# A step of a static schedule moved: the last normalisation's transposes, the router product and the routing steps stand 28 to 36 ticks later

## The chip, the cores and the metric

The kernel runs on one core of one Trainium2 chip. The metric is the device time of one execution in microseconds. Five engines work side by side, each through its own list of instructions in order: TensorE (PE, with its weight loads shown as PEld), VectorE (DVE), ScalarE (ACT), GpSimd (POOL) and SyncE (SP), which here issues most DMAs. They meet only in semaphores.

## The reference

16 sequences of 128 rows and 256 columns pass through two layers, each an attention-like mixer and a feed-forward part, all with residual additions:

```python
x = x + _L0_xattn_ref(_layernorm(x), k, bias, ctx, ctx, 8)          # long convolution of ctx * v, gated
x = x + _L0_ffn_ref(_layernorm(x), W, bias, rw1, ..., A, B, gates)  # dense + top-2 of 16 low-rank experts
x = x + _L1_xattn_ref(_layernorm(x), ctx, wq, ..., wp, bp)          # 16-head attention, q and out int8-quantised
x = x + _L1_ffn_ref(_layernorm(x), router_w, expert_bias, gate_w, up_w, down_w, shared...)
```

The last part is the one that the change is about. Each of the 2048 tokens is normalised, a router product of 32 columns gives scores sqrt(softplus(logits)), the four best of 32 experts (by score plus bias) are taken, and the output is the weighted sum of their clamped SwiGLU results plus that of a shared expert:

```python
logits = flat @ router_w.T
scores = jnp.sqrt(jax.nn.softplus(logits))
_, idx = jax.lax.top_k(scores + expert_bias, K)          # K = 4, E = 32
topv = jnp.take_along_axis(scores, idx, axis=1); topv = topv / (topv.sum(-1, keepdims=True) + 1e-20)
out = sum over e of p[:, e] * ((silu(clip(flat @ wg.T)) * clip(flat @ wu.T)) @ wd.T)  + shared expert
```

## The kernel before, in words

The work is cut into 16 blocks of 128 tokens (b = 0 to 15). A block goes through everything up to the router in one long software pipeline; then all tokens are scattered to lists by expert in HBM, gathered again as 95 tiles of 128 rows of one expert each, multiplied, scattered back and summed.

The order of the pipeline is written out by hand in tables of numbers. Every engine's program runs the same loop over ticks (t = 0 to 5785), and each step stands at a first tick and repeats at a fixed distance: 128 ticks for what is done once a block, 32 for what is done four times a block, 32 also for the shared expert (SD), and at T + GOFF[g] for the five routing groups (blocks 0 to 3, 4 to 7, 8 to 11, 12 to 14, 15; GOFF is 0, 512, 1024, 1408, 1536). Ticks are no time: they only fix the order of the steps on one engine, since each step first waits for its semaphores. Two steps of one tick stand in the order of the code.

The steps that matter here, with their lines:

- xC (DVE L796, L800) adds the attention's output to x and takes the statistics stD; rsD (POOL L1239 to L1243) makes the factor; xnD (ACT L1058) normalises; xd (ACTq L1080) writes the rows four times to HBM.
- xnTD (PE L452, L453) transposes xnD, x4 (ACT L1181) copies the result out of its PSUM bank, rp (PE L459) is the router product, lg (DVE L805) copies the logits.
- routing of a group: ra (ACT L1199, L1201: Abs, Exp), rb (DVE L836), rc (ACT L1205: Ln), rd (DVE L840 to L857), re (ACT L1209: Sqrt), top (DVE L861 to L880), mb (DVE L887 to L894), rk (PE L492, L493), cum (DVE L902 to L917), which yields the index lists ixl. Exp and Tanh, Ln, and Sqrt need different tables on ACT; the switch shows as ACT_TABLE_LOAD.
- the list (POOL L1313): 64 indirect DMAs that scatter a staged block of rows to the experts' lists. SP loads the seven staging slots (L1371) and before that fills the lists with 32 writes of 2 MB (L1350); the first load waits for all of them.
- softmax of the attention: S (PE L537), mx (DVE L791), P (ACT L1164), PP (PE L523, transposes), PT (ACT L1156, the copy), pv (PE L508, which needs PT), oT (ACT L1171), oP (PE L516), oi (DVE L779 to L627, quantiser), oiP (PE L437, L438), oiT (ACT L1176), op (PE L445).
- the long convolution: kv (POOL L1299), conv (PE L557, in a single bank), z (DVE L773), uT (PE L346, L348). The low-rank experts: pa (L375), rl (L370), wx (DVE L741), wxp (PE L382), wb (PE L388, L392), xB (DVE L747).
- the shared expert, from tick 2652 on: xr (PE L466), x5 (ACT L1186), gu (PE L478), sc (DVE L810, L813), th (ACT L1191), hh (DVE L818), dn (PE L486), acc (DVE L822).

PSUM banks are handed out in PE's order from a ring of four; a PE step waits until the reader of what was in its bank four steps before is done.

Of the kernel before, what the change touches and what calls it, by code (L numbers as in the profile page):

```python
# [93 lines left out]
def build(nc, a_x, a_ctxT, a_tk, a_pack, a_qp, a_rows, a_w, a_dest, a_pad, out):  # L94
    ctx = ExitStack()
    with ctx:
        def sb(name, shape, dt=F32):
            return ctx.enter_context(nc.sbuf_tensor(name, shape, dt))
# [24 lines left out]
        def cutter(base):  # L123
# [18 lines left out]
        z = [carve([128, 2048]) for _ in range(3)]  # L142
# [12 lines left out]
        xi = [carve([128, 256]) for _ in range(2)]  # L155
# [3 lines left out]
        v = [carve([128, 16, 32]) for _ in range(3)]  # L159
# [6 lines left out]
        x4 = [carve([128, 256]) for _ in range(2)]  # L166
# [5 lines left out]
        rb = [carve([128, 4, 256]) for _ in range(4)]  # L172
# [3 lines left out]
        th = [carve([128, 2, 128]) for _ in range(3)]  # L176
        hT = [carve([128, 128]) for _ in range(2)]
        y = [carve([128, 256]) for _ in range(4)]
        xr = [tk[:, 8 + b, :] for b in range(4)]
        x5 = [tk[:, b, :] for b in range(2)]  # L180
        sc = [tk[:, 12 + b, :] for b in range(2)]
# [8 lines left out]
        lg = [sb(f"lg{i}", [128, 80]) for i in range(2)]  # L190
# [23 lines left out]
        mb = sb("mb", [128, RG * NE], BF16)  # L214
# [4 lines left out]
        cum = sb("cum", [128, NB + 1, NE])  # L219
# [68 lines left out]

        T_PE = {"wsc": 555, "xnTA": 235, "uT": 574, "xnTB": 757, "h": 780, "rl": 802, "pa": 811, "wxp": 831,
# [3 lines left out]
        T_DVE = {"swb": 533, "mvA": 66, "sk": 400, "xA": 583, "mvB": 711, "hb": 785, "e2": 806, "wx": 813,  # L293
# [3 lines left out]
        T_ACT = {"vT": 240, "xT": 760, "eh": 783, "e2": 819, "wxT": 831, "kz": 924, "xiT": 893, "qT": 992,  # L297
            "P": 1011, "oiT": 1168, "x4": 1196, "x5": 2658, "th": 2679, "ra": 1592, "rc": 1603, "re": 1668,
            "oT": 1137, "xnA": 212, "xnB": 747, "xnD": 1190, "xd": 1196, "shw": 2459, "xr": 2571,
            "xnC": 878, "q": 923, "PT": 1035}  # L300
        T_POOL = {"rsA": 131, "rsB": 699, "rsC": 827, "rsD": 1170, "vc": 315, "us": 415, "kv": 296, "xb": 818,
# [1182 lines left out]
```

How the kernel before makes its waits and increments, by code:

```python
        def tensor_program(pe):  # L309
            pe.wait_ge(d_id, 16)
            for t in range(TICKS):
                for n in at(t, T_PE["wsc"], 16, 2):
                    p, free = banks.take(("wint", n), s_wint, n + 1)
                    pb = p[:, :].bitcast(BF16)
                    pe.wait_ge(*free)
                    pe.wait_ge(s_const, 1)
                    pe.wait_ge(s_wq, n + 1)
                    for c in range(2):
                        for k in range(2):
                            o = 256 * k + 128 * c
                            i = pe.transpose(pb[:, o:o + 128], wtb[:, 256 * c + 128 * k:256 * c + 128 * k + 128], idb[:, :])
                    i.then_inc(s_wqT, 1)
                    if n == 0:
                        continue
                    p, free = banks.take(("swb", n), s_swb, 1)
                    pe.wait_ge(*free)
                    pe.wait_ge(s_pconst, 1)
                    for c in range(2):
                        i = pe.matmul(p[:, 128 * c:128 * c + 128], ones[:, :], wdg[:, c, :], start=True, stop=True)
                    i.then_inc(s_wsc, 1)
                for b in at(t, T_PE["xnTA"], 128, NB):
                    p, free = banks.take(("vT", b), s_vT, b + 1)
                    pe.wait_ge(*free)
                    pe.wait_ge(s_xn["A"], b + 1)
                    pe.transpose(p[:, 0:128], xnA[0][:, 0:128], ident)
                    pe.transpose(p[:, 128:256], xnA[0][:, 128:256], ident).then_inc(s_xnT["A"], 1)
```

## Time and profile before

| | |
|---|---|
| three runs | 724.69, 725.38, 725.76 us (median 725.38) |
| the profiled execution | 728.71 us, its span 726.9 us |
| busy in the span | PE 579.1 us (80%), DVE 482.2 (66%), ACT 379.5 (52%), POOL 373.7 (51%) |
| PE clock granted, mean | 0.922 of full |
| HBM | 53.92 MB read, 100.28 MB written |

A profile row gives a start and a duration; what stands in brackets is how long the engine had been idle before, and what released it. A busy share is a mean over stages: the pipeline of blocks lasts to about 496 us, the rest of the list to 530, the expert tiles to 685, the summing to the end. PE's recorded durations overlap, since matmuls are pipelined: the distance of two starts is what one costs.

### The profile page before, as it was taken

To read this page: it belongs to the slowest core of one execution; us is meant where nothing else is said; L and a number is where in the kernel's file an instruction comes from. 1 tells how busy PE (TensorE), PEld (TensorE's weight loads), DVE (VectorE), ACT (ScalarE), POOL (GpSimd) and SP (SyncE) were. 2 spreads that over 40 slices of the span, in tenths; PEclk is the share of its full clock that TensorE was granted. 3 is DMA by queue.
4 is the path that set the end of the run, shared out by engine and by line. 5 is a ranking of instruction groups with operands and counts; after the bars stand their busy time and mean duration, and the time that the engine had idled before them with its cause. 6 is when DMAs were issued, how large, how long until landed. Compare 5 with 4: busy or idle time off the path is not lost.

```text
span 726.9 us, 14275 instructions
## 1 busy us (share of the span) xinstructions
PE 579.1 (80%) x4045; PEld 467.2 (64%) x4045; DVE 482.2 (66%) x1462; ACT 379.5 (52%) x1107; POOL 373.7 (51%) x526
## 2 busy tenths in 40 slices
PE   1588899999969966986998779973069999999920
PEld 1487788777758855775786556652058878888810
DVE  1646657777897753789657796677437776555587
ACT  1002456666765542782757765673036666666610
POOL 6757847564472536874316521054715555555550
PEclk9999999999988986997999989996569999999975
DMA  8989999999999964321004990269535555555688
GB/s 279 218 214 334 335 334 332 334 325 317 317 317 328 307 206 139 119 67 52 30 17 145 334 330 29 74 187 343 178 110 159 162 158 157 158 161 161 208 278 277
DMA packets 135740, 155.02 MB, mean 213 GB/s; under 512 B 15248, under 2 KB 124944, under 8 KB 135408
## 3 DMA queue, kind: packets, MB, share of 16 engines
q1 hardware_dynamic: 117536, 122.50, 56.8%
q0 software_dynamic: 7632, 20.98, 8.0%
q10 hardware_dynamic: 10496, 10.62, 4.6%
q8 instruction: 36, 0.59, 0.4%
q14 instruction: 40, 0.33, 0.2%
HBM read 53.92 MB, written 100.28 MB: 212 GB/s over the span
## 4 chain that ended last, share of the span: by engine, by line
PE 39%; SPq 31%; DMA 12%; DVE 9%; issue 4%; ACT 2%; POOL 2%; ACTq 0%; DVEq 0%; POOLq 0%
SPq L1350 28%; PE ps L605 11%; PE pS L578 6%; PE pc L557 3%; DMA stage<-in_pad 3%; DMA expert_rows<-stage 3%; DMA work<-y_rows 2%; SPq L1333 2%; PE pS L537 2%; DMA expert_rows<-stage,ixl 2%; PE ps L478 2%; PE ps L348 2%; PE ps L523 1%; PE po L597 1%; DVE xs L1048 1%
## 5 line engine op out<-in xcount | busy, mean ns | idle before, releaser
L1323 POOL DMA_INDIRECT y_rows<-tk,work x95 | 94.1, 990 | 81.8 <-ACT tk L1231 74.9
L557 PE MATMUL pc<-arena,tk 128*128 128x128 f32 x768 | 109.2, 295 | 15.8 <-DVE arena L773 8.5
L557 PEld LDWEIGHTS pc<-arena,tk 128*128 128x128 f32 x768 | 97.4, 203 | 28.7 <-DVE arena L773 15.0
L1299 POOL TENSOR_TENSOR arena<-arena 128x512 f32<-128x512 f32 x64 | 90.4, 1430 | 19.8 <-ACT arena L1099 19.5
L605 PE MATMUL ps<-arena,work 128*128 x380 | 99.8, 386 | 0.3 <-ACT work L1226 0.3
L985 DVE TENSOR_SCALAR work<-ps 128x256 f32<-128x256 f32 x95 | 40.2, 423 | 67.9 <-PE ps L605 67.3
L1313 POOL DMA_INDIRECT expert_rows<-stage,ixl x64 | 63.7, 995 | 35.6 <-DMA stage<-xn_rows 17.9
L1164 ACT ACTIVATE work<-pS,work 128x128 f32<-128x128 f32 x256 | 72.5, 370 | 3.7 <-DVE work L791 3.7
L605 PEld LDWEIGHTS ps<-arena,work 128*128 128x128 f32 x380 | 66.0, 194 | 5.9 <-issue 0.7
L578 PE MATMUL pS<-arena,tk 128*128 x190 | 59.6, 395 | 2.2 <-ACT tk L1221 2.1
L791 DVE TENSOR_REDUCE work<-pS 128x4 f32<-128x512 f32 x64 | 43.8, 685 | 26.3 <-PE pS L537 26.2
L773 DVE TENSOR_TENSOR arena<-pc,arena 128x512 f32<-128x512 f32 x64 | 43.5, 680 | 24.6 <-PE pc L557 24.6
L1216 ACT ACTIVATE tk<-work 128x128 f32<-128x128 f32 x95 | 29.4, 309 | 56.6 <-DVE work L985 51.4
L1239 POOL TENSOR_TENSOR stD<-stD,epsc 128x1 f32<-128x1 f32 x16 | 3.0, 188 | 91.1 <-DVE stD L618 91.1
L523 PE MATMUL ps<-pk,work 128*128 128x128 f32 x256 | 39.5, 277 | 3.5 <-ACT work L1164 1.5
L578 PEld LDWEIGHTS pS<-arena,tk 128*128 128x128 f32 x190 | 28.3, 188 | 19.5 <-issue 10.5
L1156 ACT ACTIVATE work<-ps 128x512 f32<-128x512 f32 x64 | 37.8, 591 | 3.1 <-PE ps L523 1.6
L1231 ACT ACTIVATE tk<-pS 128x256 f32<-128x256 f32 x95 | 37.1, 390 | 3.5 <-DMA y_rows<-tk,work 3.5
L537 PE MATMUL pS<-arena,work 32*128 32x256 f32 x256 | 37.2, 408 | 0.2 <-ACT work L1149 0.2
L348 PE MATMUL ps<-pk,arena 128*128 128x128 f32 x256 | 36.8, 295 | 0.0
L523 PEld LDWEIGHTS ps<-pk,work 128*128 128x128 f32 x256 | 30.0, 142 | 7.4 <-issue 2.1
L348 PEld LDWEIGHTS ps<-pk,arena 128*128 128x128 f32 x256 | 33.5, 156 | 0.0
(271 smaller groups left out, 1369.0 us busy)
## 6 DMA issues: line engine op xcount, KB each, us to landing
expert_rows<-stage SPq DMA_DIRECT2D x32, 2080.0 KB, 21.7
work<-expert_rows SPq DMA_DIRECT2D x95, 130.0 KB, 2.2
arena<-in_w SPq DMA_DIRECT2D x8, 1536.0 KB, 14.7
stage<-xn_rows SPq DMA_DIRECT2D x64, 130.0 KB, 2.4
xn_rows<-xnD ACTq DMA_DIRECT2D x16, 512.0 KB, 7.5
work<-y_rows SPq DMA_DIRECT2D x16, 512.0 KB, 5.2
tk<-in_tk SPq DMA_DIRECT2D x1, 2048.0 KB, 9.3
out<-xs SPq DMA_DIRECT2D x16, 128.0 KB, 3.2
```

The costliest lines, as they stand in the source:

```text
L348: i = pe.matmul(pv, zv[:, k, :], ident, is_transpose=True, start=False, stop=(k == 7))
L523: i = pe.transpose(p[:, 128 * k:128 * k + 128], Pt[m % 3][:, 128 * k:128 * k + 128], ident)
L537: i = pe.matmul(p[:, 256 * c:256 * c + 256], qT[b % 3][r, 128 * c:128 * c + 128], kz[b % 3][r, c, :, :].rearrange("p a b -> p (a b)"), sta ...
L557: i = pe.matmul(pv, tk[:, h, 128 * d:128 * d + 128], kvv[:, ci, :, :].rearrange("p b (i h j) -> p (b i) h j", i=8, h=8)[:, :, hl, :], star ...
L578: i = pe.matmul(p[U * k:U * k + U, 0:256], hT[n % 2][:, U * k:U * k + U], arena[:, 512:][:, bass.ds(e, 256)], start=True, stop=True)
L605: i = pe.matmul(p[U * k:U * k + U, 0:256], xgT[n % 3][:, 128 * c + U * k:128 * c + U * k + U], arena[:, 256 * c:][:, bass.ds(e, 256)], sta ...
L791: dve.tensor_reduce(mx[:, g, :], sbanks.place["S", m][:, :].rearrange("p (k m) -> p k m", k=4), AX.X, ALU.max, negate=True).then_inc(s_mx, 1)
L1164: i = act.activation(Pt[m % 3][:, 128 * k:128 * k + 128], sbanks.place["S", m][:, 128 * k:128 * k + 128], ACT.Exp, bias=mx[:, g, k:k + 1])
L1299: pool.tensor_tensor(kv[kk % 4][:, c, half, :].rearrange("p (i h j) -> p i h j", h=8, i=8), i0, i1, ALU.mult).then_inc(s_kv, 1)
L1313: pool.indirect_dma_start(out=Xs, out_offset=bass.IndirectOffsetOnAxis(ap=ixl[:, b, k:k + 1], axis=0), in_=stage[:, j % NS, :], in_offset= ...
L1323: pool.indirect_dma_start(out=Yr, out_offset=bass.IndirectOffsetOnAxis(ap=xg[n % NX][:, 256:257].bitcast(U32), axis=0), in_=y[n % 4], in_o ...
L1350: sp.dma_start(Xs[e * NB * 128:(e + 1) * NB * 128, :].rearrange("(j p) d -> p j d", p=128), stage[:, e % 4, :].unsqueeze(1).broadcast_to(( ...
```

## The change

Only numbers in four tables are different; no instruction is added or removed. For instance on PE:

```diff
-            "xnTD": 1196, "rp": 1201, "xr": 2652, "gu": 2663, "dn": 2738, "rk": 1724, "pv": 1038, "PP": 1025,
+            "xnTD": 1228, "rp": 1236, "xr": 2652, "gu": 2679, "dn": 2754, "rk": 1752, "pv": 1038, "PP": 1025,
```

In full: PE xnTD +32, rp +35, gu and dn +16, rk +28. DVE lg +36, sc, hh and acc +16, rb and rd +32, top, mb and cum +28, ta +30. ACT x4 +33, th +16, ra +30, rc +32, re +28. POOL and SP keep their orders; so do xnD, xd and x5 on ACT and xr on PE. xnTD moves from before the third of a block's four pv steps to before the fourth, behind uT, wxp, PP and wb.

On DVE, routing group 1, where block 8's attention output is added (xC, L796). Before:

```order
L791 TENSOR_REDUCE work<-pS1 128x4
L861 RECIPROCAL rt<-rt 128x128
L863 TENSOR_TENSOR rt<-rt 128x128
L865 TENSOR_TENSOR rt<-rt 128x128
L867 TENSOR_SCALAR rt<-rt 128x128
L869 TENSOR_TENSOR rt<-rt,rows 128x128
L873 MAX m8<-rt 128x8 x4
L877 MAX_INDEX i8<-m8,rt 128x8 x4
L880 CAST f8<-i8 128x32
L690 TENSOR_REDUCE s16_0<-arena 128x32
L704 SCALAR_TENSOR_TENSOR arena<-arena 64x128
L796 SCALAR_TENSOR_TENSOR work<-ps3,work,swb 128x256
```

After:

```order
L796 SCALAR_TENSOR_TENSOR work<-ps3,work,swb 128x256
L800 TENSOR_TENSOR xs<-xs,work 128x256
L616 BN_STATS stD<-xs 128x6
L618 BN_AGGR stD<-stD 128x2
L773 TENSOR_TENSOR arena<-pc,arena 128x16x32
L791 TENSOR_REDUCE work<-pS0 128x4
L714 SCALAR_TENSOR_TENSOR lg1<-ps3,lgb 128x16
L717 MAX lg1<-lg1 128x8
L719 TENSOR_TENSOR lg1<-lg1 128x1
L720 MAX_INDEX ix1<-lg1 128x8
L722 TENSOR_TENSOR lg1<-rows,ix1 128x32
L861 RECIPROCAL rt<-rt 128x128
```

The top-4 cluster (L861 to L880) stood between mx and xC; now xC and its statistics come first, and the cluster stands behind the top-2 choice of block 11 (L714 to L722), ahead of that block's wx.

On ACT, the same group, around the Ln of rc (L1205) and the PT copies (L1156). Before:

```order
L1199 ACTIVATE rt<-lg4 128x128
L1201 ACTIVATE rt<-rt 128x128
L1121 ACTIVATE work<-ps2 128x256
L1205 ACT_TABLE_LOAD
L1205 ACTIVATE rt<-rt 128x128
L1156 ACTIVATE work<-ps3 128x512
L1164 ACT_TABLE_LOAD
L1164 ACTIVATE work<-pS1,work 128x128 x4
L1058 ACTIVATE xnA0<-xs,stA 128x256
L1149 ACTIVATE work<-ps1,bq4,wsm 128x128 x2
L1058 ACTIVATE xnB0<-xs,stB 128x256
L1156 ACTIVATE work<-ps3 128x512
```

After:

```order
L1181 ACTIVATE work<-ps3 128x256
L1164 ACTIVATE work<-pS1,work 128x128 x4
L1058 ACTIVATE xnA0<-xs,stA 128x256
L1199 ACTIVATE rt<-lg4 128x128
L1201 ACTIVATE rt<-rt 128x128
L1149 ACTIVATE work<-ps0,bq4,wsm 128x128 x2
L1205 ACT_TABLE_LOAD
L1205 ACTIVATE rt<-rt 128x128
L1058 ACTIVATE xnB0<-xs,stB 128x256
L1156 ACTIVATE work<-ps3 128x512
```

ra, rc and the Ln table load stood before the PT copy and P of the third quarter; now they stand behind that P, around qT (L1149), ahead of xnB and the PT copy of the fourth quarter. x4 (L1181) stands directly before P.

On DVE, the quantiser oi of block 13 (L779 to L627) and the shared expert's sc (L810, L813), hh (L818) and acc (L822). Before:

```order
L818 SCALAR_TENSOR_TENSOR tk<-tk 128x128
L822 SCALAR_TENSOR_TENSOR xs<-ps2,xs 128x256
L779 RECIPROCAL work<-ps3 128x16
L781 TENSOR_TENSOR work<-ps3,work 128x256
L621 TENSOR_REDUCE work<-work 128x1
L623 TENSOR_SCALAR work<-work 128x1
L625 RECIPROCAL work<-work 128x1
L627 TENSOR_SCALAR work<-work 128x256
L791 TENSOR_REDUCE work<-pS1 128x4
L810 TENSOR_SCALAR tk<-ps3 128x256
L813 TENSOR_TENSOR tk<-tk 128x128
```

After:

```order
L627 TENSOR_SCALAR work<-xnC0,work 128x256
L810 TENSOR_SCALAR tk<-ps3 128x256
L813 TENSOR_TENSOR tk<-tk 128x128
L779 RECIPROCAL work<-ps1 128x16
L781 TENSOR_TENSOR work<-ps1,work 128x256
L621 TENSOR_REDUCE work<-work 128x1
L623 TENSOR_SCALAR work<-work 128x1
L625 RECIPROCAL work<-work 128x1
L627 TENSOR_SCALAR work<-work 128x256
L791 TENSOR_REDUCE work<-pS1 128x4
L818 SCALAR_TENSOR_TENSOR tk<-tk 128x128
L822 SCALAR_TENSOR_TENSOR xs<-ps2,xs 128x256
```

hh and acc stood before oi and sc behind it; now it is the other way round.

## Rows read from the trace of the kernel before

**Rows 1.** The chain that ended last, in order of time: start us, us, what
```profile
251.98 19.70 DMA expert_rows<-stage
...
274.61 1.19 POOL expert_rows L1313
```

**Rows 2.** Stages: us, busy of each engine, PEclk, DMA share, GB/s
```profile
303.20:335.80 32.60, 26.13 (x203) 21.52 (x203) 27.62 (x74) 20.83 (x50) 25.42 (x32) 0.91 0.28 85
...
403.00:428.80 25.80, 19.15 (x149) 14.22 (x149) 21.36 (x73) 21.32 (x53) 12.36 (x20) 1.00 1.01 381
...
456.10:474.50 18.40, 16.67 (x135) 12.09 (x132) 12.08 (x33) 11.19 (x34) 1.45 (x4) 1.00 0.24 71
474.50:495.60 21.10, 11.65 (x92) 8.62 (x93) 15.77 (x60) 13.69 (x30) 9.89 (x13) 0.96 0.79 257
495.60:530.00 34.40, 7.85 (x28) 5.45 (x28) 16.80 (x88) 5.77 (x10) 21.71 (x23) 0.55 0.70 224
```

**Rows 3.** Who waited for whom: us in total, times, longest us
```profile
PE ps L452 <- ACT xnD L1058: 18.5, 4, 12.8
```

**Rows 4.** Timeline 274 to 281 us: start us, us, instruction, [idle before <-releaser]
```profile
279.25 0.45 PE L452 MATMUL ps<-pk,xnD 128*128 128x128 f32 x1 [12.82 <-ACT xnD L1058]
...
279.84 0.65 PE L508 MATMUL po<-work 128*32 128x128 f32 x8
```

**Rows 5.** Timeline 383 to 386 us, block 10
```profile
384.42 0.57 ACT L1156 ACTIVATE work<-ps 128x512 f32<-128x512 f32 x1
...
384.65 0.30 PE L452 MATMUL ps<-pk,xnD 128*128 128x128 f32 x1
...
385.04 0.43 PE L508 MATMUL po<-work 128*32 128x128 f32 x8
```

**Rows 6.** Timeline 366 to 372 us, block 9
```profile
366.96 1.03 PE L392 MATMUL ps<-pk,work 128*128 128x256 f32 x4
...
367.92 0.42 PE L508 MATMUL po<-work 128*32 128x128 f32 x8
...
371.25 0.60 PE L523 MATMUL ps<-pk,work 128*128 128x128 f32 x4
```

**Rows 7.** Timeline of DVE, 320 to 334 us, group 1
```profile
322.47 0.94 DVE L861 RECIPROCAL rt<-rt 128x128 f32<-128x128 f32 x1
...
324.22 2.20 DVE L867 TENSOR_SCALAR rt<-rt 128x128 f32<-128x128 f32 x1
...
330.89 0.47 DVE L796 SCALAR_TENSOR_TENSOR work<-ps,work,swb 128x256 f32<-128x256 f32 x1
```

**Rows 8.** Timeline of PE, 320 to 338 us
```profile
331.41 0.61 PE L370 MATMUL ps<-pk,arena 64*128 64x16 f32 x2 [4.69 <-DVE work L796]
331.95 2.08 PE L537 MATMUL pS<-arena,work 32*128 32x256 f32 x8
```

**Rows 9.** Timeline of ACT, 306 to 320 us
```profile
309.09 1.28 ACT L1205 ACT_TABLE_LOAD   x1
310.39 0.31 ACT L1205 ACTIVATE rt<-rt 128x128 f32<-128x128 f32 x1
...
315.26 0.60 ACT L1156 ACTIVATE work<-ps 128x512 f32<-128x512 f32 x1
```

**Rows 10.** Timeline 443 to 455 us, block 13
```profile
447.61 0.25 DVE L779 RECIPROCAL work<-ps 128x16 f32<-128x16 f32 x1
...
449.69 0.30 PE L437 MATMUL ps<-pk,work 128*128 128x128 f32 x1
```

**Rows 11.** Timeline 486 to 508 us, block 15 and the list
```profile
488.55 0.75 DVE L861 RECIPROCAL rt<-rt 128x96 f32<-128x96 f32 x1
...
491.70 0.48 DVE L796 SCALAR_TENSOR_TENSOR work<-ps,work,swb 128x256 f32<-128x256 f32 x1
...
493.48 0.18 POOL L1239 TENSOR_TENSOR stD<-stD,epsc 128x1 f32<-128x1 f32 x1 [8.66 <-DVE stD L618]
...
507.44 0.95 POOL L1313 DMA_INDIRECT expert_rows<-stage,ixl  x1 [3.62 <-DMA stage<-xn_rows]
```

More of the change, by code:

```diff
@@ L290, in build @@
             "wb": 835, "kp": 924, "vp": 983, "xiP": 886, "qp": 918, "qP": 977, "oiP": 1166, "op": 1170,
[1 row of a table removed]
[1 row of a table added]
             "S": 998, "tab": 3610, "conv": 430, "oP": 1138}
         T_DVE = {"swb": 533, "mvA": 66, "sk": 400, "xA": 583, "mvB": 711, "hb": 785, "e2": 806, "wx": 813,
[2 rows of a table removed]
[2 rows of a table added]
             "tb": 3342, "tc": 3398, "td": 3400, "te": 3500}
         T_ACT = {"vT": 240, "xT": 760, "eh": 783, "e2": 819, "wxT": 831, "kz": 924, "xiT": 893, "qT": 992,
-            "P": 1011, "oiT": 1168, "x4": 1196, "x5": 2658, "th": 2679, "ra": 1592, "rc": 1603, "re": 1668,
+            "P": 1011, "oiT": 1168, "x4": 1229, "x5": 2658, "th": 2695, "ra": 1622, "rc": 1635, "re": 1696,
             "oT": 1137, "xnA": 212, "xnB": 747, "xnD": 1190, "xd": 1196, "shw": 2459, "xr": 2571,
```

4 rows, old and new, of the table T_DVE are left out of this document.

## The prediction

> **What bounds the kernel now.** I read the chain of waits in order of time first [rows 1]. It is three different stories. Up to 272 us it consists of the 2 MB writes of L1350 that fill the expert rows, one after another, and ends in the last of them landing and the first reload of a staging slot; only then can GpSimd (POOL) make its first scatter, at 274.61. From there to about 495 us it is almost all TensorE (PE), with short pieces of DVE and ACT. From 495 to 530 it is POOL's list of scatters with their DMAs, and from 533 to 685 again PE, in the expert tiles, which the change doesn't touch.
>
> The table by stage [rows 2] says what can be had between 279 and 495 us. In a stage without routing PE works 16.67 of 18.40 us: nearly full. In those with a routing group it loses 6.5 us (303 to 336), 6.6 us (403 to 429) and 9.5 us (474 to 496). In the last stage before the tiles POOL is the busy one, 21.7 of 34.4 us, and PE stands.
>
> The change slides three things in every block of 128 ticks: PE's transposes of xnD and the router product 32 and 35 ticks, with the ACT copy and the DVE copy behind them; the routing steps of each group 28 to 32 ticks; and the shared expert's gu, sc, th, hh, dn, acc 16 ticks. What matters is only what each now stands in front of and behind. POOL and SP keep their order, and ACT keeps xnD where it was.
>
> **The first 274 us: 0.** The list of waits shows 18.5 us of PE waiting at L452 for xnD [rows 3], and looks like the prize. But 12.82 of them are one wait, and it ends at 279.25, behind the fill [rows 4]. ACT is held in the same place, at xnD, and the next thing on ACT is the copy PT (L1156). With L452 out of the way PE would come to L508, which needs that very copy: it starts at 279.84 in both versions. Whatever the four blocks before gain or lose, up to about 8 us (PE stood from 266.4 to 279.25, and POOL can't give it new input before 275.8), ends in the same wait.
>
> **Conv blocks 7, 9, 10: +0.6 us.** In an ordinary block PE finishes L375, and L452 starts at 384.65; the pair takes some 0.25 us; L508 starts at 385.04, just after the PT copy of 384.42, which runs 0.57 us [rows 5]. So the pair costs nothing there: PE would have waited for PT anyway. In its new place it stands between L392 and L508, and there PE has 0.1 us free (L392 from 366.96, four passes of 0.21, L508 at 367.92) [rows 6]. Each block pays some 0.2 us, three blocks 0.6. The router product (0.36 us) goes from one full place to another. ACT's copy x4 now stands before the exponentials of L1164 and holds them back by some 1.5 us, to about 368.3, but their reader L523 comes only at 371.25 [rows 6]: covered, by 1 us in blocks with 16 conv matmuls and by almost nothing in those with 8.
>
> **Routing group 1 (303 to 352 us): -0.5 us.** What goes: DVE runs the top-4 cluster from 322.47 and comes to xC (L796) at 330.89, 8.4 us later; one of its instructions, a plain L867, takes 2.20 us [rows 7], and L880 as long. PE waits 4.69 us at L370 for the bank [rows 8] and then runs slowly: the eight score matmuls from 331.95 take 2.08 us [rows 8], twice what they take at full clock, some 1.9 us more with L375 behind them. Now xC comes before the cluster, so stall and slow stretch, 6.6 us, go.
>
> What comes instead: (1) rc with its table load stands before the PT copy. Its input rb stands behind mx on DVE, which waits for S on PE, which waits for qT on ACT, which stands behind ra. S ends at about 316.2; mx 0.7, rb 0.25, Ln 0.3, xnB 0.6 and PT 0.6 follow, so PT ends at about 319 where it ended at 315.86 (315.26 and 0.60) [rows 9]; L508 waits 2.5 us. (2) rd, 3.7 us long in this group by its own rows, moves from before xB to between xi and oi, so oi and PE's oiP come 3 to 5 us later; at L370 PE is then where it was, at 331.4, having waited elsewhere. (3) After that PE is 1.7 us early at L508 and up to 4.8 us at L382, but the cluster, mb (3.9 us) and cum (2.6 us) now lie on DVE before the z products and xB, which hold conv's single bank and vp's bank; of the lead some 0.5 us is left at 350 us. I take -0.5; the ends are -6.6 (nothing of (1) to (3) is paid) and +3.5 ((1) and (2) in full, less the 2.7 that (3) would give back).
>
> Where the Trainium skill speaks: its page "ScalarE: Activation LUTs" (What ACT_TABLE_LOAD costs) puts a switch of table at 1283 ns and a drain of about 1380 ns. The trace has a load of 1.28 us at 309.09, and the activation it serves starts right behind it [rows 9], with no drain. By the page the four switches of a group would be 2.66 us each and the two of them that now stand before xnD and PT in group 2 would cost 2.8 us more than below, a sum of +5.4; I go by the row.
>
> **Routing group 2 (403 to 443 us): +0.5 us.** The 6.6 us that PE loses before come from the same things in small: the Ln load before PT, rd before xB, the tanh load before oiT. They go. In their place PT waits for rc (2.7 us), oi waits for rd (2.9 us), and re's Sqrt load plus the tanh reload, 2 x 1.28 us, stand right before the PT copy that releases L508 at 429. The sum over the stage is -0.7 us if PE keeps its clock and +1.5 if it doesn't; before, it stood at full in this stage [rows 2] and fell behind it. Nearest the middle: +0.5. Ends -3.0 and +3.2.
>
> **Blocks 13 and 14: +2.6 us.** This is the term that carries the forecast. Before, DVE goes from L822 straight to oi (L779 at 447.61), and PE's L437 takes the result at 449.69; the gu product (L478) fills the gap [rows 10]. After, DVE has sc (L810, L813) in front of oi, and sc needs gu, which on PE now stands behind oP and xiP. PE's oP ends at about 446.9, gu runs to 448.4, sc to 449.4, oi takes its 1.93 us to 451.4: L437 starts at about 451.55, 1.9 us late, with PE idle for about 2.0 us before it. Part comes back, since S and gu have moved apart and the wait for oT is filled differently: I count +1.3 a block, two blocks 2.6. Ends 0 and +4.1 (2 x 2.05, nothing back). Block 12 is in group 2, block 15 in the last term.
>
> **Block 15 and the list: -0.6 us.** POOL stands 8.66 us, to 493.48, for block 15's statistics, and everything to 529.9 follows from there: 23 scatters of 1.26 us, once held 3.62 us by a slot's reload [rows 11]. DVE reached xC at 491.70, after a 3.1 us cluster begun at 488.55. PE's op was ready at 489.4, so the cluster's move is worth 2.2 us; but oi of block 15 waits for gu 12 and sc 12 as above (+1.6 us). xC comes at 491.1: -0.6. The index list of group 3 becomes ready 4 us later than before (501.5), still before its first scatter at 506.8; that of group 4 about when needed. Ends -3.1 (whole cluster) and +1.9 (late list of group 4).
>
> **Sum.** 0 + 0.6 - 0.5 + 0.5 + 2.6 - 0.6 = +2.6 us. The profiled execution took 728.71 us (span 726.9) and would take 731.3; it is 3.3 above the median of the three runs, 725.38, so the median becomes 728.0.
>
> **Rivals.**
> A, faster: with the top cluster behind xC the long stalls simply go. 4.69 us at L370 and 2.2 us at xC 15, less the 0.6 of the pair and 1.3 for one block of late oi: -5.0, 720.4 us. For it: these are the longest single waits in [rows 8] and [rows 11]; the slow 2.2 us instructions fell where POOL was multiplying without pause, and at 335 us, where the cluster goes, POOL is nearly done. Against: rd goes to where POOL is busy. It wins if oi isn't held by rd and sc. (The Trainium skill's page "SBUF — State Buffer", Who interferes with whom, says DVE's fast modes and GpSimd lock each other out for a whole instruction; the 2.20 us [rows 7], against 0.23 of the same instruction in group 2, agree.)
> B, no change: DVE's clusters only trade places, and what PE wins at one wait it loses at the next; or the list with its slots starts and ends as before. 725.4, within 1.4. For it: PE is near full outside the routing stages.
> C, much slower: PT behind rc costs 3 us in both groups and the idle time drops PE's clock (0.55 in the stage from 495.6 [rows 2] shows what standing does): 6 us for these and 1 us for slow matmuls on top of the other terms near zero, 732.4. It decides from the point where rb is released only by S.
>
> **Chances.** My forecast, slower by 1.5 to 5 us: 0.38. A 0.29, B 0.23, C 0.10. About 0.2% (1.45 us) can be told from no change here. So faster 0.29, same 0.23, slower 0.48. The forecast's own range is 726.9 to 730.5; with A and C taken in until a fifth is left out, 721.5 to 732.
>
> **What would show it.** PE's L452 in the new place with no wait, and L508 before it still released by L1156. At L370 no long wait in group 1. L508 at about 319 us held by ACT L1156 for 2 to 3 us. In blocks 12 to 15 PE waiting 1 to 2 us at L437 for DVE L627, with L810 and L813 just ahead of L779. POOL's last wait for stD ending 2 us later than before. The forecast is wrong if PE reaches S of block 13 no later than before, or if stD of block 15 comes 3 us earlier.

## The result: 24 us slower

| | before | after |
|---|---|---|
| median (4 runs each, one chip) | 725.57 us (724.69 to 725.93) | 749.37 us (748.86 to 754.22) |
| ratio | | 1.0345, 95% interval 1.0301 to 1.0389 |
| profiled execution, span | 728.71, 726.9 us | 749.71, 747.9 us |
| PE busy, clock granted | 579.1 us, 0.922 | 586.4 us, 0.910 |

I forecast 728.0 us, range 721.5 to 732.0. Slower was right; the size was wrong by a factor of nine: +23.8 us where I had +2.6.

The quickest way to see where a pipeline loses time is to take one event of each block and subtract. I take the start of L618, the statistics stD at a block's end. "Period of block 8" is the distance from block 7's L618 to block 8's.

```
block             5     6     7     8     9    10    11    12    13    14    15
before         26.2  24.8  36.9  31.5  25.8  24.2  18.4  25.3  26.7  19.5  21.0
after          29.2  27.3  22.8  37.1  27.0  24.5  18.7  25.0  38.3  21.8  23.3
```

stD of block 7 comes at 300.89 before and 299.55 after; of block 15 at 493.21 and 515.28, 22.1 us later. From there to the end after is 1.1 us shorter, which makes the 21.0 between the two profiled executions. Two periods carry most: block 13 (+11.6) and block 8 (+5.6). What blocks 4 to 7 gain and lose cancels, as the first scatter shows.

Blocks 4 to 6 lost 13.1 us, so that stD of block 6 came 12.7 us late (263.99 before, 276.73 after). Before, POOL waited 12.79 us at its first scatter, for the reload behind the fill ([rows 1]); after, there is no such wait. The first row is of before, the second of after:

```profile
274.61 1.19 POOL L1313 DMA_INDIRECT expert_rows<-stage,ixl  x1 [12.79 <-DMA stage<-xn_rows]
...
273.31 1.19 POOL L1313 DMA_INDIRECT expert_rows<-stage,ixl  x1 [0.60 <-issue]
```

The slack behind the fill was about 13 us, and it was used up almost to the last.

Stages of after, by blocks 8 and 12 to 15 (columns as in [rows 2]):

```profile
299.55:336.70 37.15, 27.46 (x204) 22.93 (x203) 24.49 (x52) 18.22 (x47) 23.80 (x29) 0.86 0.25 76
406.86:431.86 25.00, 18.24 (x133) 13.90 (x133) 14.72 (x48) 17.48 (x47) 11.43 (x18) 0.86 0.97 359
431.86:470.12 38.26, 26.94 (x163) 19.79 (x162) 22.61 (x88) 17.36 (x46) 3.53 (x8) 0.78 0.25 83
470.12:491.95 21.83, 16.78 (x144) 12.95 (x143) 11.24 (x33) 13.10 (x39) 2.74 (x5) 1.00 0.20 61
491.95:515.28 23.33, 14.88 (x101) 11.42 (x101) 12.40 (x39) 12.66 (x30) 9.60 (x12) 0.77 0.71 234
```

Block 13 of before:

```profile
425.98:452.65 26.67, 23.66 (x157) 17.61 (x156) 19.78 (x70) 13.57 (x40) 3.54 (x8) 0.87 0.37 124
```

Of block 13's 11.6 us, 8.3 are time in which PE is not busy (11.3 against 3.0) and 3.3 are PE being slower at what it does (26.9 against 23.7 busy). The granted clock was 0.78 on average: half of full from 439.8 to 450.1 and from 456.9 to 463.7 us, full between. Before each of the two falls PE had stood for 3.0 to 3.3 us (the rows of block 13 below).

**Group 1 (block 8).** In before, the cluster of rd stood here, with oi (L779) five microseconds behind it:

```profile
310.73 0.76 DVE L840 TENSOR_SCALAR rt<-rt 128x128 f32<-128x128 f32 x1 [1.34 <-ACT rt L1205]
...
314.21 0.23 DVE L857 TENSOR_SCALAR rt<-rt 128x128 f32<-128x128 f32 x1
...
319.41 0.26 DVE L779 RECIPROCAL work<-ps 128x16 f32<-128x16 f32 x1 [0.77 <-PE ps L516]
```

DVE, POOL and PE of after:

```profile
318.04 1.40 POOL L1299 TENSOR_TENSOR arena<-arena 128x512 f32<-128x512 f32 x1 [2.78 <-ACT arena L1099]
319.51 0.21 DVE L840 TENSOR_SCALAR rt<-rt 128x128 f32<-128x128 f32 x1
...
320.64 1.43 POOL L1299 TENSOR_TENSOR arena<-arena 128x512 f32<-128x512 f32 x1
321.14 1.08 DVE L847 TENSOR_TENSOR rt<-rt 128x128 f32<-128x128 f32 x1
...
322.58 2.24 DVE L851 TENSOR_TENSOR rt<-rt 128x128 f32<-128x128 f32 x1
323.27 1.40 POOL L1299 TENSOR_TENSOR arena<-arena 128x512 f32<-128x512 f32 x1
...
325.19 3.52 DVE L857 TENSOR_SCALAR rt<-rt 128x128 f32<-128x128 f32 x1
325.87 2.75 POOL L1299 TENSOR_TENSOR arena<-arena 128x512 f32<-128x512 f32 x2
...
328.63 0.24 DVE L779 RECIPROCAL work<-ps 128x16 f32<-128x16 f32 x1
329.39 0.90 PE L363 MATMUL ps<-arena,pk 128*64 128x128 f32 x3 [7.01 <-DVE work L781]
```

rd's cluster runs from 319.51 to 328.63, 9.1 us; I had taken 3.7, its duration in its old place. Three of its instructions (L847, L851, L857) end 0.1 to 0.2 us after a product of POOL (L1299) ends. In group 2, where POOL makes no products, rd takes 3.2 us in both kernels. oi (L779) stands behind it, PE waits 7.01 us. The stall that I had expected to go is gone: L370, which waited 4.69 us [rows 8], and the score matmuls behind it run without a wait, at full speed:

```profile
336.63 0.39 PE L370 MATMUL ps<-pk,arena 64*128 64x16 f32 x2
336.95 1.13 PE L537 MATMUL pS<-arena,work 32*128 32x256 f32 x8
```

The stall has changed its name, it is longer (7.01 us), and PE comes to L370 5.2 us later than before. The wait of PT behind rc is there too, at 1.8 us where I had 2.5 (against [rows 9]):

```profile
315.92 0.31 ACT L1205 ACTIVATE rt<-rt 128x128 f32<-128x128 f32 x1 [0.84 <-DVE rt L836]
316.62 0.57 ACT L1156 ACTIVATE work<-ps 128x512 f32<-128x512 f32 x1
317.25 0.66 PE L508 MATMUL po<-work 128*32 128x128 f32 x8 [1.82 <-ACT work L1156]
```

**Block 13.** The long waits of after, in order, with the DVE and ACT rows that they are put down to:

```profile
433.94 1.28 ACT L1209 ACT_TABLE_LOAD   x1
...
436.32 1.28 ACT L1191 ACT_TABLE_LOAD   x1
...
438.46 0.43 PE L508 MATMUL po<-work 128*32 128x128 f32 x8 [3.04 <-ACT work L1156]
...
443.91 1.22 PE L486 MATMUL ps<-tk 128*128 128x256 f32 x2 [1.34 <-DVE tk L810]
...
446.63 1.91 PE L392 MATMUL ps<-pk,work 128*128 128x256 f32 x4
...
453.08 0.86 DVE L902 TENSOR_TENSOR cum<-ps,cum 128x32 f32<-128x32 f32 x4
...
456.03 0.65 PE L523 MATMUL ps<-pk,work 128*128 128x128 f32 x4 [3.31 <-DVE work L761]
457.16 2.07 PE L537 MATMUL pS<-arena,work 32*128 32x256 f32 x8
457.26 0.31 ACT L1191 ACTIVATE tk<-tk 128x128 f32<-128x128 f32 x1 [4.07 <-PE ps L486]
```

Read it as three links. re's and th's table loads stand before a PT copy: 3.0 us. mb stands before sc, so dn (L486) waits 1.3 us. cum stands before v (L761), whose bank PP needs: 3.3 us; dn is behind that PP, and th, on ACT before the next PT, waits 4.07 us for dn. L392 takes 1.91 us where four passes took 1.03 [rows 6], L537 2.07 instead of 1.13: they fall into the stretches of half clock. The three links are read from one trace; the runs below test parts of them, none tests each alone.

From the list of waits, all of the span:

```profile
POOL stD L1239 <- DVE stD L618: 132.1, 16, 19.4
...
PE po L508 <- ACT work L1156: 23.6, 22, 3.4
...
PE ps L363 <- DVE work L781: 11.3, 2, 7.0
```

**The end.** The start of the last stage follows block 15, and the list then has one wait of 3.55 us, for group 4's indices, in place of the slot wait in [rows 11]. L437 is the row that my forecast had named:

```profile
511.87 0.45 PE L437 MATMUL ps<-pk,work 128*128 128x128 f32 x1 [1.51 <-DVE work L627]
...
515.55 0.19 POOL L1239 TENSOR_TENSOR stD<-stD,epsc 128x1 f32<-128x1 f32 x1 [11.10 <-DVE stD L618]
...
529.53 0.96 POOL L1313 DMA_INDIRECT expert_rows<-stage,ixl  x1 [3.55 <-DVE ixl L917]
```

### The profile page after: what moved, and what is told of

It is laid out like the page before. It is cut to its first block, busy times and chain, and to the rows that moved or that the text cites. A ratio compares the mean times of both kernels' runs of the same rounds, so it can differ in the third digit from the quotient of the medians.

```text
span 747.9 us, 14279 instructions
## 1 busy us (share of the span) xinstructions
PE 586.4 (78%) x4045; PEld 474.0 (63%) x4045; DVE 484.1 (65%) x1462; ACT 380.8 (51%) x1107; POOL 372.9 (50%) x526
## 4 chain that ended last, share of the span: by engine, by line
PE 56%; DVE 20%; issue 7%; DMA 6%; POOL 5%; ACT 4%; ACTq 0%; SPq 0%; DVEq 0%; POOLq 0%
PE ps L605 10%; PE pc L557 10%; PE pS L578 5%; PE pS L537 3%; PE po L508 3%; POOL arena L1299 3%; DMA work<-y_rows 2%; PE ps L348 2%; PE ps L523 2%; PE ps L388 2%; PE ps L392 2%; PE ps L478 2%; PE ps L409 2%; DMA expert_rows<-stage,ixl 2%; DVE work L627 1%
## 5 line engine op out<-in xcount | busy, mean ns | idle before, releaser
L557 PE MATMUL pc<-arena,tk 128*128 128x128 f32 x768 | 113.4, 303 | 15.7 <-DVE arena L773 8.4
L557 PEld LDWEIGHTS pc<-arena,tk 128*128 128x128 f32 x768 | 101.6, 210 | 28.9 <-issue 14.4
L1299 POOL TENSOR_TENSOR arena<-arena 128x512 f32<-128x512 f32 x64 | 90.0, 1423 | 27.1 <-ACT arena L1099 26.9
L1216 ACT ACTIVATE tk<-work 128x128 f32<-128x128 f32 x95 | 29.4, 310 | 55.8 <-DVE work L985 51.8
L508 PE MATMUL po<-work 128*32 128x128 f32 x512 | 29.3, 304 | 24.5 <-ACT work L1156 23.6
L523 PE MATMUL ps<-pk,work 128*128 128x128 f32 x256 | 39.3, 277 | 5.1 <-DVE work L761 3.3
L1156 ACT ACTIVATE work<-ps 128x512 f32<-128x512 f32 x64 | 37.8, 590 | 7.5 <-PE ps L523 5.4
L537 PE MATMUL pS<-arena,work 32*128 32x256 f32 x256 | 37.2, 408 | 0.9 <-ACT work L1149 0.9
L508 PEld LDWEIGHTS po<-work 128*32 128x32 f32 x512 | 10.5, 112 | 41.6 <-ACT work L1156 33.0
L523 PEld LDWEIGHTS ps<-pk,work 128*128 128x128 f32 x256 | 30.6, 143 | 7.3 <-DVE work L761 3.6
```

The lines of the kernel that those rows point to most:

```text
L508: i = pe.matmul(po[32 * k:32 * k + 32, 128 * g:128 * g + 128], v[b % 3][:, h, :], PT[m % 3][:, 128 * k:128 * k + 128], start=True, stop=True)
L523: i = pe.transpose(p[:, 128 * k:128 * k + 128], Pt[m % 3][:, 128 * k:128 * k + 128], ident)
L537: i = pe.matmul(p[:, 256 * c:256 * c + 256], qT[b % 3][r, 128 * c:128 * c + 128], kz[b % 3][r, c, :, :].rearrange("p a b -> p (a b)"), sta ...
L557: i = pe.matmul(pv, tk[:, h, 128 * d:128 * d + 128], kvv[:, ci, :, :].rearrange("p b (i h j) -> p (b i) h j", i=8, h=8)[:, :, hl, :], star ...
L1299: pool.tensor_tensor(kv[kk % 4][:, c, half, :].rearrange("p (i h j) -> p i h j", h=8, i=8), i0, i1, ALU.mult).then_inc(s_kv, 1)
```

## The experiments

My theory after the result (theory 1): the loss is a sum of places, of the routing's first half (ra, rb, rc, rd) in front of oi, of its second half (re, top, mb, rk, cum) in block 13, and of the shared expert. The rivals: only the meeting of routing and shared expert costs (theory 2); or the moved pair (xnTD, rp, with x4 and lg) costs (theory 3). All kernels move steps and leave nothing out.

The runs fell on five further chips. On two of them the kernel before itself took 734.0 and 730.7 us (medians), and every trace shows engines standing 1 to 11 us with the releaser given as "issue" or "remote", near 405 us and after 499 us. So totals are compared through the ratio to before on the same chip, and periods only where no such wait falls in them (* marks those where one does, or falls just before). Even so one block's period is not exact: the two traces of before differ by 1.6 us in block 9 and 2.6 in block 13.

```
block                         8     9    12    13    14    15   ratio (95%)
before, first trace        31.5  25.8  25.3  26.7  19.5  21.0
before, second trace       31.5  24.1  25.5  24.1  19.5  21.0
routing, first half        37.5  24.6  29.9  24.1  19.5  20.5   1.0088 (1.0066-1.0110)
routing, second half       26.2  28.6  23.0  32.4  19.5  18.8   1.0021 (1.0008-1.0033)
routing, both              37.5  28.1  31.0* 31.2  19.5  22.5*  1.0233 (1.0184-1.0282)
shared expert              31.5  25.7  27.7* 29.3  21.9  27.1   1.0145 (1.0110-1.0180)
routing + shared           37.0  29.1  26.2* 36.9  23.2  25.6*  1.0357 (1.0309-1.0405)
the changed kernel         37.1  27.0  25.0  38.3  21.8  23.3   1.0345 (1.0301-1.0389)
```

**Four parts, on the first of these chips.** The tables of the parts, against before:

```diff
 routing:  DVE  rb 1606->1638  rd 1618->1650  top 1675->1703  mb 1683->1711  cum 1725->1753  ta 3280->3310
           ACT  ra 1592->1622  rc 1603->1635  re 1668->1696   PE  rk 1724->1752
 shared:   PE   gu 2663->2679  dn 2738->2754   ACT  th 2679->2695
           DVE  sc 2663->2679  hh 2711->2727  acc 2744->2760
 pair:     PE   xnTD 1196->1228  rp 1201->1236   ACT  x4 1196->1229   DVE  lg 1201->1237
```

Routing only: 

> Only the routing steps (ra, rb, rc, rd, re, top, mb, rk, cum, ta) are moved 28 to 32 ticks; xnTD, rp, x4, lg and the shared expert stay. Theory 1 (the loss is a sum of places, and the routing steps carry most of it: rd falls before oi where GpSimd multiplies, re and cum fall before PT and before v): +5.5 to +8 us in group 1 and +3 to +6 in group 2, so 734 to 740 us. Theory 2 (no part is dear by itself; it is the meeting of group 2's routing with the shared expert's chain gu, sc, th, hh, dn that costs): about +6 in group 1, nothing in group 2, 730 to 732. Theory 3 (the transposes of xnD carry the loss, since they wait for L696's bank): 725 to 728.

Measured 1.0198 (1.0143 to 1.0253).

Shared only: 

> Only the shared expert's steps (gu, dn, sc, hh, acc, th) are moved 16 ticks. My prediction's term for them was +2.6 in blocks 13 and 14 with +1.6 in block 15: 728 to 730 us. Theory 2 (they cost only together with group 2's routing): 726 to 730. A rival (th now stands before PT on ScalarE and waits for dn, which stands behind PP on TensorE, 4 times a block, whatever the routing does): some 1 us each, 12 or more of them, 735 to 740.

Measured 1.0204 (1.0139 to 1.0270).

Routing and pair: 

> As the changed kernel, but the shared expert's steps stay at their old ticks (gu of block 15 alone is 16 ticks later, behind its transposes). Theory 1: group 1 as in the changed kernel (+7), group 2 some +4, nothing more in blocks 14 and 15: 737 to 741 us. Theory 2: 732 to 734. If the pair's move or the routing is the whole loss: 747 or more.

Measured 1.0296 (1.0236 to 1.0356).

Routing and shared: 

> As the changed kernel, but xnTD, rp, x4 and lg stay at their old ticks. Theories 1 and 2: the pair costs 0.6 us, so 747 to 749 us. Theory 3 (the pair in its new place waits for the bank of L696 at L452 and its copy x4 holds the exponentials, some 1.5 us in every block with routing): 740 us or less.

Measured 1.0417 (1.0355 to 1.0480).

In microseconds each was dearer than theory 1 said; by the ratio, routing only is at the upper end of what it said, and the runs with two parts are above it. Shared only came out close to its own rival, th in front of PT. But before took 734.0 us here, and PE alone stands 11 to 15 us of these traces in the "issue" and "remote" waits. The totals are inconclusive; the periods that are free of them are not: shared only has block 13 at 29.3 and block 14 at 23.5, routing only block 13 at 32.8 and block 8 at 36.8. So each of the two parts is dear by itself, against theory 2, and with the pair in its old place the loss is there, against theory 3 as the whole cause.

**Before again, and the routing by halves.**

> The kernel before, unchanged, for a trace from the same chip as the runs beside it. In the four runs so far engines stood for several microseconds with the releaser given as issue or remote (2.17 us before L445 at 405.31 in the run with only the shared expert moved), while 1.5 MB weight loads ran, and the kernel before took 734 instead of 725 us. If this belongs to the chip, its trace shows such waits too, 8 us of them after 400 us, and the periods of blocks 8 to 10 are those of the first trace (31.5, 25.8, 24.2 us). If the chip is as the first one: 725 us, no such waits.

Measured 723.34 us in this one execution (the median of 13 others on this chip was 727.85), none of those waits above 0.64 us. That they don't belong to a kernel is shown better by two kernels that ran on both kinds of chip: behind 280 us, PE, DVE and ACT together stand 31 us in such waits of 0.9 us and more in the changed kernel on one chip and not at all on another; with only the shared expert moved it is 42 us and 3 us.

```diff
 first half alone:   ra, rb, rc, rd late; re, top, mb, rk, cum as before
```

> Only the first half of the routing (ra, rb, rc, rd) moves 30 to 32 ticks. Theory: in group 1 rd's eight DVE instructions now run while GpSimd multiplies (L1299), take about 9 us instead of 3.7, and stand before oi, so stD of block 8 comes 5 to 7 us later (period 36 to 38 us), and in group 2, where GpSimd does not multiply, the cost is 0 to 2 us; block 13's period stays within 1 us of 26.7: +6 to +8 in all. Rival (the second half carries the loss): group 1 within 2 us of before.

Measured 1.0088, +6.4 us, as the theory said: block 8's period is 37.5 and block 13's 24.1. In block 12, where I had allowed 2, it is 29.9 instead of 25.5; PE waits 2.1 us longer there and has a granted clock of 0.72 instead of 0.88. The rows of block 8:

```profile
326.10 3.54 DVE L857 TENSOR_SCALAR rt<-rt 128x128 f32<-128x128 f32 x1
...
330.31 1.12 PE L363 MATMUL ps<-arena,pk 128*64 128x128 f32 x4 [7.75 <-DVE work L781]
```

```diff
 second half alone:  re, top, mb, rk, cum, ta late
+    rb, rd:  at(t, T_DVE["rb"] + GOFF[g] + 32 * (g == 4), 1, 1)
```

> Only the second half (re, top, mb, rk, cum, ta) moves 28 ticks; rb and rd of the last group go 32 ticks down so that they stay behind cum of the group before. Theory: xC comes before the top-4 cluster, group 1 gains 2 to 5 us (the 4.69 us stall at L370 goes); in group 2 re's two table loads stand before PT, and mb and cum fall into block 13, whose period grows by 4 to 6 us; in all within 3 us of before. Rival: it is slower in group 1 too, by 3 us or more, because mb and cum now hold the DVE in front of xA and v.

Measured 1.0021 (1.0008 to 1.0033). Both halves of the theory are there, with other sizes: block 8 gains 5.3 us, the stall at L370 is gone and nothing takes its place (PE idles 1.1 us in the block, 6.5 before), but block 9 loses 4.5 us, so that group 1 gains only 0.8; and block 13 loses 8.3 us where the theory had 4 to 6. In block 9 PE waits for xnD; in block 13 for wx (L741) and lg (L805), which stand behind top and mb:

```profile
331.52 0.45 PE L452 MATMUL ps<-pk,xnD 128*128 128x128 f32 x1 [3.91 <-ACT xnD L1058]
...
431.15 0.47 PE L466 MATMUL ps<-pk,tk 128*128 128x128 f32 x1 [1.99 <-DVE arena L741]
...
433.87 1.11 PE L523 MATMUL ps<-pk,work 128*128 128x128 f32 x4 [1.61 <-DVE lg L805]
```

**rd moved on, behind xC** (the changed kernel, rd 1650 to 1690).

> The changed kernel with rd moved 40 ticks further, from before oi to behind xC. Theory (rd before oi is what group 1 pays): the 7.01 us wait of TensorE at L363 for DVE goes, group 1 gives back 4 to 7 us against the changed kernel; re then waits for rd and holds the PT copy behind it by 2 to 3 us in groups 1 and 2; about 3 us faster than the changed kernel in all. Rival (not rd but the waits of PT behind rc and re carry it): no better, or slower than the changed kernel by 2 to 4 us.

Measured 1.0389 (1.0366 to 1.0411), no faster than the changed kernel's 1.0345 (1.0301 to 1.0389, another chip): the total is the rival's. The place is the theory's: block 8 gives back 6.4 us (30.7) and the wait at L363 is gone, so rd before oi is what block 8 pays. But blocks 9 and 13 grow by 3.7 and 3.4 us: re waits for rd and holds PT. In block 9:

```profile
338.22 0.31 ACT L1209 ACTIVATE rt<-rt 128x128 f32<-128x128 f32 x1 [3.62 <-DVE rt L857]
...
339.56 0.65 PE L508 MATMUL po<-work 128*32 128x128 f32 x8 [4.98 <-ACT work L1156]
```

**The shared expert.** Again, on a chip where before took 726.7:

> Only the shared expert's steps moved, a second time. On the first chip it stood in stalls that its releaser names issue or remote (2 to 5 us each, near 405, 430, 500 and 525 us), so its 1.0204 says little. Theory (its own cost is what the undisturbed periods show: 4 us each in blocks 13 and 14, some 1 to 3 in block 12 and 3 in block 15): 1.010 to 1.016, 735 to 739 us. Rival (it costs only what I forecast, 2 us): 1.003 to 1.006. If the stalls come with this order and not with the chip: 1.02 again, with the same waits at L445 near 405 us.

Measured 1.0145, +10.5 us. Its block 15, 27.1 us against 21.0, has a lower clock as well (0.76 against 1.00):

```profile
478.60:505.70 27.10, 18.28 (x103) 13.97 (x101) 15.28 (x55) 13.93 (x31) 9.63 (x12) 0.76 0.73 249
```

Which of its steps is it? th back behind P (th 2711 instead of 2695):

> As the run beside it, but th (the Tanh on ScalarE) stands 16 ticks further, behind P as before, not in front of the PT copy. Theory (th in front of PT waits for sc and for dn of two rows before, and with it PT, pv): the period of block 14 falls back from about 23.5 to 19.5 to 21 us, and the whole is 6 us or more faster than the run beside it. Rival (the order sc before oi on DVE, or gu behind oP on TensorE, carries it, as I forecast): within 2 us of the run beside it.

Measured 1.0134 (1.0104 to 1.0165), within 2 us of the run beside it: the total is the rival's. Block 15 falls from 27.1 to 22.2 and block 14 from 21.9 to 21.1, but block 13 rises from 29.3 to 32.9. No longer wait does that. Block 13 of the run beside it and of this one:

```profile
427.40:456.60 29.20, 22.69 (x167) 17.37 (x166) 19.81 (x69) 14.60 (x43) 3.53 (x8) 0.94 0.24 79
...
425.60:458.40 32.80, 27.05 (x167) 20.89 (x165) 19.98 (x69) 14.40 (x43) 3.54 (x8) 0.78 0.28 89
```

PE does the same 167 matmuls in 27.05 us instead of 22.69 and stands 0.8 us less: the rise is busy time alone, at a granted clock of 0.78 instead of 0.94. So what th's place saves may be hidden in this total. And gu back between PP and pv (gu 2663, the rest late):

> Of the shared expert's steps dn, sc, hh, acc and th move 16 ticks, gu stays between PP and pv. Theory (gu was what TensorE did while ScalarE copied PT; behind pv it leaves that gap empty, and TensorE waits at L508 about 1 us each time): 0.5 to 1 per cent less than with gu moved too (1.0145), 1.004 to 1.010, and the waits at L508 for L1156 in blocks 14 and 15 (5.5 us there) fall under 3. Rival (th in front of PT and dn behind PP are enough): 1.0145 within its interval, the waits at L508 as they were.

Measured 1.0122 (1.0088 to 1.0156), above the 1.004 to 1.010 of the theory and within the rival's. PE's wait at L508 in blocks 14 and 15 did fall, from 5.5 to 1.2 us; but gu's result now holds its bank until the late sc has read it, and PE stands at the next step that needs it:

```profile
429.54 0.61 PE L424 MATMUL ps<-wint,work 128*128 128x256 bf16 x2 [6.04 <-DVE tk L810]
```

Neither step is the cause alone. The traces point to the order of gu and sc, with the bank that holds gu's result between them, but no run moved sc, hh, dn and acc apart, so this is not shown.

**Only top and mb late.**

> Only top and mb on DVE move 28 ticks; re, rk, cum and the rest stay. Theory 1 (in block 13 the cost comes from top and mb standing in front of wx, lg and sc, and from cum in front of v): blocks 8 and 12 gain as in the run with the second half (5.3 and 2.5 us), block 9 and block 13 lose 3 us and 5 us: 0.997 to 1.002. Theory 2 (the two table loads of re in front of the PT copy carry block 13's loss): blocks 9 and 13 within 1.5 us of before, 0.988 to 0.993, 719 to 723 us.

Measured 1.0076 (1.0041 to 1.0111), above both theories. Its theory 2, that re's table loads carry block 13's loss, is out: blocks 9 and 13 are at 29.6 and 29.4, not within 1.5 us of before. For its theory 1 the gains are missing: block 8 is 30.2 where the second half has 26.2, and rk, left in its place on PE, waits for mb, in block 9 for 5.09 us (the row) and in block 13 for 1.82. Block 13's 5.3 us show that top and mb cost there without re's table loads; they can't be split from rk's wait, so what re and cum add to the 8.3 of the second half stays open.

```profile
341.60 0.26 PE L492 MATMUL ps<-mb,bef 128*128 128x128 bf16 x1 [5.09 <-DVE mb L893]
```

**Does it add up?** Three runs side by side, on the chip where before took 730.7 us:

> Only the routing steps, a second time, because the first chip stalled. Both halves alone made 1.0088 and 1.0021. Theory (the halves do not add: with rd before oi the first half's 7 us wait at L363 takes the place where the second half's xC before the cluster gained 5.3 us, while the second half's losses in blocks 9 and 13 stay): group 1 +8 us and block 13 +8 us against an undisturbed trace of before, 739 to 743 us, 1.016 to 1.022. Rival (they add): 1.009 to 1.013.

Measured 1.0233 (1.0184 to 1.0282).

> Everything but xnTD, rp, x4 and lg moved, a second time. Theory (routing and the shared expert about add, and the pair's move costs 0 to 2 us): 747 to 751 us, 1.028 to 1.033. Rival (the pair's new place saves, as 1.0417 here against 1.0345 of the changed kernel would say): 754 us or more, 1.038 or more.

Measured 1.0357 (1.0309 to 1.0405).

> The changed kernel itself, on the chip of the runs beside it. 1.0345 again within its interval (1.030 to 1.039) if the chip is as the first two undisturbed ones; the difference to the run beside it is the price of the pair.

Measured 1.0440 (1.0372 to 1.0508).

This chip stalls too (5 to 6 us of "issue" before PE's L499, at 543 to 553 us, in all three traces), so the totals run high again; the first two lie above what the theory gave, and the third above its first measurement. The halves don't add: in block 8 both together take 37.5 us, just what the first half takes alone, and the second half's 5.3 us gain is not there, while its losses in blocks 9 and 13 are. In block 13 the parts do add: 24.1 + 8.3 (second half) + 5.2 (shared) = 37.6, measured 36.9 without the pair and 38.3 with it, with 2.6 us of spread in that block.

The pair's own price stays open; it was never moved alone. Side by side on one chip, moving it made +7.1 us (749.47 for routing, 756.56 for routing and pair, with gu of block 15 late as well) and +3.7 us (758.46 and 762.14); the only comparison in its favour, 1.0345 against 1.0417, is across chips. Both chips are those that stall. In blocks 8, 9, 10, 13 and 14, which are free of those waits, the pair makes +1.6 and -0.8 us.

**Versions that might beat both.** The second half late, except in group 2:

```diff
-                for g in (g for g in range(NG) for _ in at(t, T_DVE["top"] + GOFF[g], 1, 1)):
+                for g in (g for g in range(NG) for _ in at(t, T_DVE["top"] + GOFF[g] + 28 * (g != 2), 1, 1)):
```

and the same for mb, cum, rk, re; ta is late, and rb and rd of the last group as above.

> The second half of the routing (re, top, mb, rk, cum) moves 28 ticks in groups 0, 1, 3 and 4 but not in group 2. Theory (each group is its own sum: group 1 -0.8, block 15 -2.3, and group 2's net +5.8 is not paid): 3 to 5 us under the kernel before, 0.993 to 0.996, if the end of the list follows block 15. Rival (the list of group 3, now later, holds the scatters, or the gain is lost in the next waits): within 1.5 us of before.

Measured 723.84 us against 726.74: 0.9963 (0.9943 to 0.9983), 2.9 us faster than before on this one chip. Block 8 is 26.2, block 9 28.6, blocks 12 and 13 as before, block 15 20.0. The gain is small and rests on one chip: blocks 8 and 9 together make 0.8 of it, the second trace of before is as short (721.5 us, 722.0 here), and the two versions built on it, on other chips, are not clearly faster than before. Those two are tries at the wait of 3.9 us at L452 that it keeps:

> As the version with the second half late in all groups but group 2 (0.9963), and xnTD, rp, x4, lg moved 32 to 36 ticks for blocks 4 and 8 alone, where TensorE waited 3.9 us at L452 for xnD. Theory (this wait is TensorE's own loss, since POOL makes xnD's factor only after its multiplications and L346, L348 behind L452 could run meanwhile): 2 to 3 us faster still, 0.991 to 0.994. Rival (the wait only moves to L508, which needs the PT copy behind xnD on ScalarE, as I argued for block 7): 0.996.

Measured 0.9985 (0.9960 to 1.0011), on a chip that stalls. The rival was right in kind: the wait is at L508 instead, 3.9 us in block 9, as long as it was.

> The version with the second half late in all groups but group 2, and GpSimd's rsD of blocks 4 and 8 placed 27 ticks earlier, in front of two of the convolution's products (L1299), so that xnD does not wait for them. Theory: the 3.9 us wait of TensorE at L452 falls to about 1.2 and block 9's period from 28.6 to about 26: 0.992 to 0.994. Rival (the products that now come later hold the convolution or DVE by as much): 0.996 to 0.998.

Measured 1.0011 (0.9993 to 1.0030), worse than both theory and rival. The wait fell to 1.15 us, but block 9's period rose to 31.1. wx (L741) is not later: it ends 10.2 us behind stD of block 8 in both versions. PE only reaches its reader L382 sooner, waits 3.59 us there and 1.78 us at L388, and then runs at half clock (L388 takes 2.08 us where it took 1.03).

```profile
327.61 0.30 PE L452 MATMUL ps<-pk,xnD 128*128 128x128 f32 x1 [1.15 <-ACT xnD L1058]
...
335.47 0.30 PE L382 MATMUL ps<-pk,arena 128*128 128x128 f32 x1 [3.59 <-DVE arena L741]
```

## Why the prediction was wrong, point by point

- **The first 274 us, 0: right, by luck in part.** The mechanism was right (L508 starts at 279.45 after, where I had 279.84), but blocks 4 to 6 lost 13.1 us, which I had not worked out, and stD of block 7 still came 1.3 us earlier. By the bound that I gave (8 us of slack) some 5 us should have been paid; 13 were there, all used. Group 0's rd took 8.0 us instead of 3.1, the same fault as in group 1, and cost nothing for this reason alone.
- **Conv blocks, +0.6: right** where it can be read: block 10's period is 0.3 longer.
- **Group 1, -0.5: the first large miss.** Periods of blocks 8 and 9: +5.6 and +1.3, 6.9 us (against the second trace of before +5.6 and +2.9). The step that failed is (2), "rd, 3.7 us long in this group by its own rows". The rows were those of its old place. In the new one it takes 9.1 us. I had the evidence for that: L867 at 2.20 us [rows 7], and I wrote in rival A that "rd goes to where POOL is busy", but did not put it in the sum. With 9 us in place of 3.7 the term would have been near +5 (my estimate: -0.5 and the 5.4 us of difference). The other half of (2), that at L370 "PE is then where it was, at 331.4, having waited elsewhere", was right in kind, PE having waited at L363, but it came at 336.6. So the 6.6 us that I credited were not there.
- **Group 2, +0.5, and blocks 13 and 14, +2.6: the largest miss.** Block 12 came out at -0.3, block 13 at +11.6, block 14 at +2.3 (I had 1.3). I priced re's loads and rc before PT, but in this group never followed what top, mb and cum now stand in front of on DVE: wx, lg, sc and v. Their first readers are on PE. This term I had put at nothing without a reason; the second half alone costs 8.3 us in block 13. I left block 12 out of the shared expert's term as "in group 2", and priced the shared expert through one reader, oi; gu, sc, th, PT and the bank ring were not followed, and it costs 5.2 us in block 13 alone. The step that fails here is "the term that carries the forecast", +1.3 a block from oi behind sc: L437, where it was to be paid, holds PE for 0.2 and 0.6 us in blocks 13 and 14.
- **Block 15, -0.6: wrong sign, +2.3.** The cluster's gain was sized well: the second half alone gives 2.2 there (21.0 to 18.8). The shared expert alone takes 6.1, part of it clock, where I had 1.6.
- **The clock.** I priced a drop only in the upper half of group 2's term and in case C. In block 13 it is 0.78, and PE's busy time 3.3 us longer.
- **The cases.** Rival A's mechanism is real (the long stall goes, -5.3 us in block 8, of which 4.5 come back in block 9), for the second half alone; its condition, that oi isn't held by rd, did not hold. B fits none of the large stages. C's waits are there at 1.8 and 3.0 us, with a drop of the clock, but its 7 us are a part of the loss only. What I named to look for, 1 to 2 us at L437, is 0.2, 0.6 and 1.5 us in blocks 13 to 15: the loss stands at L508, L523 and L486.

What the range lacked was any case in which several small terms fail on the same side. Each was rounded toward a trade of one wait for another.

## What to carry to other kernels

When a cluster of instructions moves in a static order, its length has to be taken from its new neighbours, not from its old rows, and the list of what it now stands in front of has to be followed to the first reader on the busiest engine, all the way, for each engine. A gain from one moved step and a loss from another in the same block don't add: the later wait hides the earlier one, so test halves one by one; a part that did not lose (the second half, without group 2) was inside a change that lost 24 us. When a step that fills an engine's gap is moved, look too at who holds its bank afterwards: gu put back into the gap took 4.3 us off the waits there and met a wait of 6 us for the bank. And a block whose waits are unchanged can still be 3.6 us slower at a lower clock, so compare busy time and idle time apart.

## What was not expected of the hardware

- Plain DVE instructions of 128x128 that take 0.23 to 0.29 us took 1.08, 2.24 and 3.52 us beside POOL's products of 1.4 us: they end when a product ends, or two. In its old place, beside one product, the same cluster took 3.7 us; in group 2, with no product beside it, 3.2. The Trainium skill's page "SBUF — State Buffer" (Who interferes with whom) says that the port pair which DVE and GpSimd share is held under an exclusive lock; the traces agree: each of the slow ones ends 0.1 to 0.2 us after a product does.
- Between chips the medians of the kernel before lay between 725.6 and 734.0 us. On two of the six chips engines stood 1 to 11 us at a time in waits that no semaphore explains ("issue", "remote"), mostly at the same steps in all kernels. One of them, in the run of both routing halves:

```profile
408.18 0.36 ACT L1110 ACTIVATE arena<-ps,pk 64x128 f32<-64x128 f32 x1 [1.58 <-remote]
...
409.21 0.38 PE L445 MATMUL ps<-wint,work 128*128 128x256 bf16 x2 [1.95 <-issue]
```

What causes them was not settled.

- The same kernel's block 13 took 26.7 us in one execution and 24.1 in another, the granted clock being 0.87 and 0.99: 1.8 us of the 2.6 are PE's busy time (23.7 and 21.9), the rest is idle time.
